# A scan and attention kernel on one core: the second norm with tokens on partitions, b and c in two parts, one product on another engine, weights loaded in parts, new orders

## What is computed

```
mod = (silu(c) @ wmod).reshape(16, 6, 1, 256);  sa, ca, ga, sb, cb, gb = mod[:, 0..5]
h = layernorm(x) * (1 + ca) + sa
xz = h @ W_in.T;  xs, z = split(xz)                      # 512 channels each
B, C = xs @ W_B.T, xs @ W_C.T                            # 16 states each
dt = softplus(xs @ W_dt.T + b_dt)
state[t] = exp(dt[t] * A) * state[t-1] + dt[t] * B[t] * xs[t]      # 512 channels x 16 states
y = (sum over states of state * C + xs * D) * silu(z)
x1 = x + ga * (y @ W_out.T) * sigmoid(output_gate)
h2 = layernorm(x1) * (1 + cb) + sb                       # "the second norm"
for l in 0, 1: h2 = attention layer(h2)                  # qkv, rotary, 128-wide windows, wo,
                                                         # shifted layernorm, w1, gelu gate, w2
out = x1 + gb * h2
```

## Time and profile before

| | |
|---|---|
| median of 3 runs | 4182.83 us (4182.79 to 4183.98) |
| the profiled execution, its own time | 4186.23 us |
| its span, first to last instruction | 4184.4 us, 61077 instructions |
| busy: PE / DVE / ACT / POOL | 95% / 87% / 66% / 64% of the span |
| scan phase | 40 to 1751 us |
| second phase | 1752 to 4184 us |
| mean granted clock of PE | 0.982 of full speed |

### The profile page before, as it was taken

The page is one execution under the profiler, slowest core; times in us unless marked ns, Lnnn a source line. Parts: engine busy times, 40 slices in busy tenths (PEclk is TensorE's granted clock), DMA queues, the critical chain, the costliest instruction groups (busy, mean ns, idle before and its releaser), DMA issues.

```text
span 4184.4 us, 61077 instructions
## 1 busy us (share of the span) xinstructions
PE 3982.3 (95%) x19870; PEld 2670.8 (64%) x19870; DVE 3624.9 (87%) x6114; ACT 2743.5 (66%) x5896; POOL 2670.3 (64%) x1298
## 2 busy tenths in 40 slices
PE   7999999999999999769999999999999999999997
PEld 4444444444444444347887778787777878777785
DVE  5999999999999999768888888877888887878884
ACT  6677777777777775336767676666767666666764
POOL 3999999999999999553434444443534444343442
PEclk8999999999999999879999999999999999999998
DMA  3333333333333333420000000001110101000010
GB/s 109 117 124 124 122 122 121 122 121 121 122 122 123 125 122 116 137 91 27 21 26 17 31 16 31 16 31 51 36 63 21 41 21 37 26 31 32 21 36 26
DMA packets 119610, 295.11 MB, mean 71 GB/s; under 512 B 21288, under 2 KB 45664, under 8 KB 119296
## 3 DMA queue, kind: packets, MB, share of 16 engines
q1 hardware_dynamic: 117424, 291.15, 21.1%
q10 hardware_dynamic: 1872, 0.05, 0.0%
HBM read 248.52 MB, written 42.64 MB: 70 GB/s over the span
## 4 chain that ended last, share of the span: by engine, by line
PE 51%; DVE 2%; ACT 1%; DMA 1%; issue 1%; POOL 1%; SPq 0%; DVEq 0%; ACTq 0%; POOLq 0%
PE b_bank L1346 12%; PE b_bank L1474 12%; PE b_bank L1495 6%; PE b_bank L1425 5%; PE b_bank L1398 5%; PE b_bank L1409 5%; PE b_bank L1439 4%; PE b_bank L1378 3%; DMA b_hx<-stack_rows 1%; PE b_bank L1446 1%; ACT b_probs_t L1586 0%; DVE b_hx_part L1728 0%; DVE b_qk_rot L1773 0%; PE b_bank L1510 0%; POOL b_scores L1704 0%
## 5 line engine op out<-in xcount | busy, mean ns | idle before, releaser
L824 POOL TENSOR_TENSOR a_state<-a_state,a_c_wide 128x1024 f32<-128x1024 f32 x512 | 1195.1, 2371 | 19.7 <-DVE a_state L766 19.7
L1704 POOL TENSOR_TENSOR b_scores<-b_scores,b_row_rate 128x1024 f32<-128x1024 f32 (+1 forms) x256 | 458.2, 1801 | 825.6 <-DVE b_row_rate L1825 825.6
L584 PE MATMUL a_y_sum<-a_state,a_ident 128*128 128x512 f32 x2048 | 951.2, 597 | 6.8 <-POOL a_state L824 6.8
L766 DVE TENSOR_TENSOR_SCAN a_state<-a_decay,a_slot 128x1024 f32<-128x1024 f32 x352 | 788.7, 2270 | 0.7
L1346 PE MATMUL b_bank<-b_w_qkv,b_hx_part 128*128 128x512 f32 x2304 | 604.8, 408 | 29.9 <-DVE b_hx_part L1728 9.1
L584 PEld LDWEIGHTS a_y_sum<-a_state,a_ident 128*128 128x128 f32 x2048 | 387.3, 191 | 383.0 <-issue 316.7
L1677 POOL TENSOR_TENSOR b_by_cos<-b_qk,b_rotary 128x1024 f32<-128x1024 f32 x128 | 310.2, 2424 | 475.5 <-DVE b_qk L1757 473.4
L1474 PE MATMUL b_bank<-b_hn_part,b_w 128*128 128x512 f32 x2112 | 526.2, 399 | 7.0 <-DVE b_hn_part L1728 6.9
L695 ACT ACTIVATE a_decay<-a_dt,a_neg_a 128x512 f32<-128x512 f32 x704 | 453.8, 710 | 114.5 <-DVE a_state L766 114.1
L1574 ACT ACTIVATE b_scores<-b_scores,b_row_bias 128x256 f32<-128x256 f32 (+1 forms) x1024 | 478.2, 472 | 69.4 <-DVE b_row_bias L1814 69.4
L1346 PEld LDWEIGHTS b_bank<-b_w_qkv,b_hx_part 128*128 128x128 f32 x2304 | 428.3, 192 | 128.8 <-issue 16.4
(11 more groups left out here) (211 smaller groups left out, 6946.2 us busy)
## 6 DMA issues: line engine op xcount, KB each, us to landing
a_c_wide<-bc_rows SPq DMA_DIRECT2D x256, 512.0 KB, 3.8
a_b_wide<-bc_rows SPq DMA_DIRECT2D x80, 512.0 KB, 4.8
b_hx<-stack_rows SPq DMA_DIRECT2D x64, 256.0 KB, 3.9
b_x_res<-stack_rows SPq DMA_DIRECT2D x32, 512.0 KB, 3.4
a_xt<-in_L_attn_x SPq DMA_DIRECT2D x16, 512.0 KB, 5.4
x_rows<-a_x_t SPq DMA_DIRECT2D x16, 512.0 KB, 5.4
stack_rows<-a_h_t SPq DMA_DIRECT2D x16, 512.0 KB, 5.3
stack_rows<-b_xc SPq DMA_DIRECT2D x16, 512.0 KB, 2.9
```

Source lines behind the costliest of these rows:

```text
L584: last = nc.tensor.matmul(y_sum[dd][:], ident[:], state[state_ring.slot[q]][:, i, :], start=False, stop=(j == GROUPS - 1 and i == GROUP - 1))
L766: nc.vector.tensor_tensor_scan(flat(h), flat(factor), flat(term), 0.0, ALU.mult, ALU.add).then_inc(scan_done.sem, 1)
L824: nc.gpsimd.tensor_tensor(h[:], h[:], c_wide[c_ring.slot[q // 2]][:], ALU.mult).then_inc(cmul_done.sem, 1)
L1704: nc.gpsimd.tensor_tensor(probs, probs, row_rate[:, w, at].unsqueeze(2).to_broadcast([P, 4, hi - lo]), ALU.mult)\
```

## The change

1. **The second norm** has tokens on partitions now. PE turns x1 in PSUM (`turn_tail`, sixteen 128-column transposes for both ways), ScalarE copies with an accumulated sum (`copy_tail`), squares with an accumulated sum, takes ln and exp of a 128x4 tile (`statistics_tail`) and normalises (`normalise_tail`); PE turns back (`turn_back_tail`), ScalarE modulates from PSUM. The averages on PE and both VectorE passes are gone.
2. **b and c in two fp32r parts**, 64 rows: `bcrest` and `bcmid` are gone, `picks` is fp32r.
3. **Unit 9** is made by VectorE (TO_VECTOR): its b is spread by PE, its decay goes to SBUF. Unit 8, of the same load, stays on GpSimd.
4. **The cut of dt** moves from GpSimd to ScalarE (step `cut`).
5. **The first norm** works in place in xt: it waits until x is turned, and the first sequence's normalisation comes behind the setup's barrier.
6. **Second phase:** the q, k and v thirds of layer 1's weights are loaded one by one, each when the last product of layer 0 with that third is done; w_1 and w_2 are loaded in `load_hx` of sequence 18, behind its hx. ORDER, BANK_OF, FIRST_ORDER and MIXER_ORDER are new.

```diff
...
+TO_VECTOR = 9
...
-    for part in range(3):
+    for part in range(2):
...
-    1: "xload xT xcopy stat norm hT mod up hcut xs xscopy bc bccopy cstore bcup bcrest bcmid bclow dt soft dtadd"
-       " z zcopy silu",
+    1: "xload xT xcopy stat norm hT mod up hcut xs xscopy bc bccopy cstore bcup bclow dt soft dtadd"
+       " z zcopy silu cut",
     0: "skip bcast cload bload decay mul scan cmul sum gate",
-    -1: "out res x1store mean2 cen2 sq2 var2 dev2 xn2 h2 h2store"}
+    -1: "out res x1store turn2 tot2 stat2 norm2 hT2 h2 h2store"}
...
-scan-:10 scan-:11 cmul-:6 cmul-:7 scan-:12 scan-:13 bcast-:13 bcmid-:0 xT-:1 xs-:0 xscopy-:3 xs-:1 decay-:19 soft-:0
...
+mul-:28 sum-:27 decay-:24 mul-:29 decay-:25 decay-:26 cmul-:26 bcast-:31 scan-:28 xload:0 sum-:28 cmul-:27 dt-:1
...
-        picks = sb("picks", [P, STATES, P], BF16)
+        picks = sb("picks", [4 * STATES, STATES, P])
...
-        by_pool = [q for q in units if q // 2 in POOL_LOADS]
+        by_pool = [q for q in units if q // 2 in POOL_LOADS and q != TO_VECTOR]
...
-            normalise_head_of(act, 0)
...
+            wait(act, x_turned, s, CHUNKS)
             wait(act, shift_done, s, TILES)
             for t in range(TILES):
-                nc.scalar.activation(xn[:, t, :], xt[:, t, :], ACT.Identity, bias=token_shift[:, t:t + 1],
+                nc.scalar.activation(xt[:, t, :], xt[:, t, :], ACT.Identity, bias=token_shift[:, t:t + 1],
                                      scale=token_rate[:, t:t + 1]).then_inc(xn_done.sem, 1)
...
-                    last = nc.tensor.matmul(slots[q % 2][:, i, :], picks[0:96, GROUP * j + i, :], bc_parts[slot][0:96, :],
+                    last = nc.tensor.matmul(slots[q % 2][:, i, :], picks[:, GROUP * j + i, :].bitcast(F32R), bc_parts[slot][:].bitcast(F32R),
...
+            def turn_tail(s, slot, i):
                 wait(pe, x1_done, s, CHUNKS)
...
+                banks.wait_free(pe, s, f"turn2{i}")
+                for t in (2 * i, 2 * i + 1):
+                    for c in range(CHUNKS):
+                        at = (t % 2) * DIM + c * P
+                        last = nc.tensor.transpose(bank(f"turn2{i}")[:, at:at + P], x1_t[:, c, t * P:(t + 1) * P], ident[:])
+                last.then_inc(x1_turned.sem, 1)
+
+            def turn_back_tail(s, slot, c):
+                wait(pe, xn2_done, s, TILES)
+                banks.wait_free(pe, s, f"hT2{c}")
+                for t in range(TILES):
+                    last = nc.tensor.transpose(bank(f"hT2{c}")[:, t * P:(t + 1) * P], xn2[t][:, c * P:(c + 1) * P], ident[:])
+                last.then_inc(h2_turned.sem, 1)
...
+                nc.scalar.activation(bc_parts[slot][0:2 * STATES, :].bitcast(F32R), bank("bc0")[0:2 * STATES, :], ACT.Copy).then_inc(parts_upper.sem, 1)
...
+            def cut(s, slot, half):
+
+                wait(act, u_done, s, half + 1)
+                nc.scalar.activation(dt[slot][:, 2 * half:2 * half + 2, 0:1], half_cut[:], ACT.Copy, scale=2.0).then_inc(dt_done.sem, 1)
...
+            def copy_tail(s, slot, i):
+                wait(act, h2_turned, s - 1, CHUNKS)
+                wait(act, x1_turned, s, i + 1)
+                for t in (2 * i, 2 * i + 1):
+                    at = (t % 2) * DIM
+                    nc.scalar.activation(xn2[t], bank(f"turn2{i}")[:, at:at + DIM], ACT.Copy, accum_out=neg_mean2[:, t:t + 1])\
+                        .then_inc(total2_done.sem, 1)
+
+            def statistics_tail(s, slot, _):
                 wait(act, h2_stored, s - 1, 1)
...
+                wait(act, total2_done, s, TILES)
+                nc.scalar.activation(neg_mean2[:], neg_mean2[:], ACT.Copy, scale=-1.0 / DIM).then_inc(mean2_done.sem, 1)
+                wait(act, mean2_done, s, 1)
+                for t in range(TILES):
+                    nc.scalar.activation(squares2[t], xn2[t], ACT.Square, bias=neg_mean2[:, t:t + 1],
+                                         accum_out=token_rate2[:, t:t + 1]).then_inc(var2_done.sem, 1)
+                wait(act, var2_done, s, TILES)
+                nc.scalar.activation(token_rate2[:], token_rate2[:], ACT.Ln, scale=1.0 / DIM, bias=ln_eps[:]).then_inc(var2_done.sem, 1)
+                wait(act, var2_done, s, TILES + 1)
+                nc.scalar.activation(token_rate2[:], token_rate2[:], ACT.Exp, scale=-0.5).then_inc(rate2_done.sem, 1)
+
+            def normalise_tail(s, slot, _):
+                wait(act, rate2_done, s, 1)
...
+            def modulate_tail(s, slot, c):
+                wait(act, h2_turned, s, c + 1)
+                modulate(s, h2_t[:, c, :], bank(f"hT2{c}"), MOD_SHIFT_B, MOD_SCALE_B, c).then_inc(h2_done.sem, 1)
...
+            def lower_bc(s, slot, _):
+                wait(dve, bc_done, s, 1)
                 wait(dve, parts_upper, s, 1)
...
+                nc.vector.tensor_tensor(bc_parts[slot][2 * STATES:, :].bitcast(F32R), bank("bc0")[0:2 * STATES, :],
+                                        bc_parts[slot][0:2 * STATES, :], ALU.subtract).then_inc(parts_done.sem, 1)
...
-                wait(pool, u_done, s, half + 1)
-
-                nc.gpsimd.tensor_tensor(dt[slot][:, pair, 0:1], half_cut[:], half_cut[:], ALU.add).then_inc(dt_done.sem, 1)
...
-ptr-:3 v-:3 hxs:0 mask:1.0 vc-:3 mask:1.1 score:0.0 score:0.1 score:1.0 hxload:0 exp:0 rate:0 add:0 pss:0 score:1.1
...
+onorm-:3 ptr-:3 att-:3 mask:0.0 mask:0.1 score:0.0 score:0.1 score:1.0 exp:0 psq:0 score:1.1 hxs:0 hxload:0 mask:1.0
...
-pss:0 pnorm:0 prot:0 padd:0 pq:0 pk:0 v:0 pss:1 psq:0 prate:0 vc:0 psq:1 prate:1 ptc:0 pnorm:1 pk:1 prot:1 vc:1 vc:2
...
+pq:0 psq:0 pk:0 pss:0 pnorm:0 prate:0 vc:0 prot:0 v:0 psq:1 prate:1 padd:0 pss:1 pnorm:1 vc:1 pk:1 prot:1 v:1 pq:1
...
-            def load_qkv():
-
-                for i, done in enumerate(qkv_loaded):
-                    at = slice(i * INNER, (i + 1) * INNER)
-                    for to, source in zip(w_qkv, parts_dram["qkv"]):
-                        sp.dma_start(to[:, :, at], source[:, :, at]).then_inc(done, 16)
+            def load_qkv(i):
+
+                at = slice(i * INNER, (i + 1) * INNER)
+                for to, source in zip(w_qkv, parts_dram["qkv"]):
+                    sp.dma_start(to[:, :, at], source[:, :, at]).then_inc(qkv_loaded[i], 16)
...
-                if s < 3 or s == BATCH:
+                if s < 3:
...
-                    load_qkv()
+                    sp.wait_ge(q_full.sem, q_full.at(s - 1, TILES))
+                    load_qkv(0)
+                    sp.wait_ge(k_full.sem, k_full.at(s - 1, TILES))
+                    load_qkv(1)
+                    sp.wait_ge(v_done.sem, v_done.at(s))
+                    load_qkv(2)
                     sp.wait_ge(by_cos_done.sem, by_cos_done.at(s))
                     sp.wait_ge(by_sin_done.sem, by_sin_done.at(s))
                     sp.dma_start(rotary[:], rotary_dram).then_inc(rotary_moved, 16)
+                if s == BATCH + 2:
+                    sp.wait_ge(h2_done.sem, h2_done.at(BATCH))
+                    load_w_1()
+                    sp.wait_ge(x_out_done.sem, x_out_done.at(BATCH))
+                    for to, source in zip(w_2, parts_dram["w_2"]):
+                        sp.dma_start(to[:], source).then_inc(w_2_loaded, 16)
...
-                if s == BATCH - 1:
-                    sp.wait_ge(h2_done.sem, h2_done.at(BATCH))
-                    for done, group in zip(moved, (early, late)):
-                        sp.wait_ge(done, 3 * loads_of(group))
-                    load_w_1()
                 sp.wait_ge(x_out_done.sem, x_out_done.at(s, CHUNKS))
                 sp.dma_start(stack_dram[s + BATCH], x_out[:]).then_inc(stored.sem, 16)
-                if s == BATCH - 1:
-                    for to, source in zip(w_2, parts_dram["w_2"]):
-                        sp.dma_start(to[:], source).then_inc(w_2_loaded, 16)
...
-                nc.vector.tensor_copy(picks[0:96], pick[0:96].unsqueeze(2).to_broadcast([96, STATES, P]))
+                nc.vector.tensor_copy(picks[:].bitcast(F32R), pick[0:4 * STATES].unsqueeze(2).to_broadcast([4 * STATES, STATES, P]))
...
```

192 lines of the change are left out of this document (74 added, 118 removed).

## The result

| | before | after |
|---|---|---|
| median of 4 runs | 4182.81 us | 4239.38 us (4233.92 to 4242.63) |
| the profiled execution's span | 4184.4 us | 4240.8 us |
| interval of a sequence | 103.33 us | 109.77 us |
| first to last logarithm of the second phase's norm, 31 intervals | 2233.4 us | 2190.0 us |

The ratio is 1.0135, 95% interval 1.0117 to 1.0152: slower by 56.6 us, where I forecast 41 us less. The two traces say where (times of the two profiled executions, spans 56.4 us apart): the first Silu starts 4.3 us later, fifteen sequences take 96.6 us more, the last Silu to the first product of the second phase 3.4 more; then the second phase gives back 3.9 at its start, 43.4 in 31 passes and 0.6 at its end.

The account below looks back on a forecast made before the run. VectorE, with GpSimd level, was taken to bound the scan phase, TensorE the second. Terms -23 + 4.5 - 8.3 - 2.5 - 3 - 6 - 2 = -40.3 from 4186.2 us, less 3.4 to the median: 4142 us, range 4114 to 4172.

Parts of the forecast that it names:

- the waits for spreads: Scan phase, sign of being wrong: VectorE waits for spreads or decays by more than 0.5 us per sequence.
- the step of 0.3: Scan phase, sign of being wrong: TensorE's fp32r spreads step by more than 0.3 us.
- the longer passes: Second phase, sign of being wrong: passes take longer than 71.7 us.
- Rival D: Scan phase: TensorE becomes the bound, slower from a spread step of 0.335 us; at 0.43, +66 us, 4231; chance 0.07.
- Scan phase, VectorE: VectorE, without slack at 103.3 us per sequence, loses norm passes and a subtraction, gains a product: net -1.7, to 101.6.
- Its gain of 1.43 us per sequence: Scan phase: the interval falls by 1.73 us less 0.3 of new waits, times 16 sequences: -23 us.
- rival A: Scan phase: later spreads or decays hold VectorE another 1.4 us per sequence, taking the 23 us gain: 4165; chance 0.15.
- GpSimd: Scan phase: GpSimd falls from about 103 to 100.2 us per sequence, no longer level with VectorE, which sets the interval.
- Ends of the scan phase: First normalisation +3.3, path through b and c -1.9, longer serial ScalarE norm about +3: +4.5 us (0 to +9).
- Weights, -8.3 and -2.5: Second phase: stall at layer 1's q, k, v load gone, -8.3 us; wait for hx behind w_1 and w_2, -2.5.
- Orders: Second phase's new order: -3 us for hx waits, -6 for the mean's wait for probabilities, -2 in the first pass.
- B: Second phase rival: the new order costs one microsecond in each of 32 passes and the mean's 6: 4180; chance 0.10.

Follow-up runs that it names:

- e1: The changed kernel with the spread of b padded from 64 to 96 rows with zeros, still fp32r: 4136.84 us, 0.9888 of before.
- e5: e1 with one of the three products of the scan phase's two-part projections left out: 4141.57 us, 0.9904 of before.
- e3: The kernel before with the whole new second phase (orders, banks, weight loads): 4135.09 us, 0.9884 of before.
- e6: e1 with the product of unit 9 back on GpSimd: 4166.55 us, 0.9966 of before.
- e8: The kernel before with only the second phase's new orders and banks, old weight loads: 4134.61 us, 0.9885 of before.
- e4: The kernel before with only the new loads of layer 1's weights, old orders: 4175.54 us, 0.9981 of before.
- e9: The changed kernel, still 64 rows, with the pattern and the two parts of b in bf16: 4191.57 us, 1.0022 of before.

## Why the prediction was wrong, step by step

- **The step that failed**: "How an fp32r spread with 64 rows and a 0/1 pattern steps is in no row. Lower bound 0.215, upper bound 0.43, I take 0.24." The product does step by 0.235. Missing is the term for the two ends of each stretch, 0.20 and 0.19 us. I had read the length of the load (187 ns) and charged 0.05 for its later end; what counts is where it starts. TensorE's work rose by 7.5 us per sequence, where I had no rise (98.8 to 98.7), and its room before was 3.6 us and not 4.5. Of the signs that I had named, the waits for spreads came (5 us per sequence, where 0.5 was the mark); the step of 0.3 and the longer passes did not.
- **Rival D** was this outcome in its mechanism (TensorE becomes the bound), its place and nearly its time (4231 against 4239), with 0.07. I argued against it with fp32r products "at full width and depth", which is just what a 64-row spread is not. Its price was put on the product instead of on the change of height, so its threshold of 0.335 could not be judged from any row. That its time came so near is luck: it had 70 us of loss in the scan phase and 22 of gain in the second, where 104 and 48 were measured.
- **Scan phase, VectorE**: the sums were right. In e1, where height is taken out, VectorE's steps at their medians add up to 101.5 us, as forecast: both norm passes and one subtraction gone, one product more.
- **Its gain of 1.43 us per sequence** did not come even in e1: 103.40. VectorE's idle time rose from 0.3 to 1.2 us per sequence, where I charged 0.3 more, and some of its steps came out longer than the median. That is rival A, once height is out of the way; what holds it there is open after e5. So the scan phase's rewrite, even without the 64 rows, gained nothing: e3, with the scan phase of before, takes 4135.09 us and e1 4136.84.
- **GpSimd** fell below VectorE as forecast (101.57 of 110 busy after). I took the moved product as a cost to VectorE that GpSimd's relief merely allowed; e6 shows it to be worth 2.1 us in the new order.
- **Ends of the scan phase**: +4.5 forecast, +7.7 measured: 4.3 at the first Silu instead of 1.4, 3.4 at the end instead of 3. Neither bears out its term. Before, e3 and e8 share one scan phase, and their first Silu starts at 68.2, 69.8 and 70.8 us, so up to 2.6 of the 4.3 can be spread between runs. And in e1 the end, from the last Silu to the first product of the second phase, takes 136.1 us against 137.1 before: the 3.4 goes with the height, and the 3 for ScalarE's longer norm met it by luck.
- **Weights, -8.3 and -2.5**: e4 gives -8.2 for both with the old orders; how that divides between them no trace shows. With the new orders the stall would have been gone anyway. I added two edits that remove the same wait.
- **Orders**: -3 for hx, -6 for the mean, -2 for the start, 11 in all; e8 shows 47 with the stall's 8 in it. Small waits for hx fell from 5.8 to 0.6 us and the mean's waits went, near the forecast. What I did not count is what a busy TensorE hides: 0.4 us per pass in exposed loads at the scores, and 0.26 in the row of sixteen turns besides the wait behind it. (Ahead of the mean stand sixteen score products, not the eight of the prediction.) I had written that in the second phase "only what TensorE waits for counts", with 74.75 of 75 busy; loads that are not covered count as busy there.
- **The chances**: half of B's 0.10 is 0.05, where the sum took 0.04; it changes nothing.

## What to carry to other kernels

Lay the row of weight loads beside the row of products and compare starts, not lengths: a load that starts with its product can be on the path, and the steps on both sides, added up, say whether it is. Do this wherever the height or the width of neighbouring products differs, and price a change of shape by what stands before and behind it; padding with zero rows can be the faster form. On an engine that a page shows as 99% busy there can still be one per cent of exposed loads and short waits (0.96 of 71.7 us per pass here), and a handmade order with a fixed map of banks loses them again with one step moved. Test each part of a change by itself: here one part lost 102 us, another gained 47, and a third gained nothing.

## What the runs showed of the hardware

- Products of 64 rows between products of 128: load exposed at both ends, 0.20 us at the start and 0.19 at the end in fp32r, 0.10 and 0.19 in bf16 (e9). Each end costs about the load that stands there: the spread's own at the start (185 ns in fp32r, 94 in bf16), that of the fp32 sums behind it at the end (190). 96 rows among 128: not exposed, in bf16 or in fp32r (e1). Further products of the stretch are not charged. Into products of 128 rows that are 64 columns wide the load starts with its product too (second phase of before). The load's length does not depend on the height: 185 ns for 64 rows, 190 for 96 and for 128 in fp32r and fp32. On that the Trainium skill agrees, in "TensorE: Matmul & The Clock Gate", section on LDWEIGHTS: columns count, not rows. Its section "The mechanism" says that a load is pulled ahead when its row group does not conflict or when it goes to the background weight buffer, and in its list of what overlaps it says that a load overlaps with running products only when the row groups differ. The rows here differ from that list: between 128-row products in the same rows the load leads by 0.23 us, and it is at a change to or from 64 rows that it does not. Why 64 rows prevent it and 96 do not, no run here shows.
- With 6 us less work per sequence, and idle for 12 of 200 us instead of 6.6, TensorE was granted a lower clock in the scan phase (0.97 for 0.99, more stretches at 1.2 GHz among those at 2.4), and the kernel was not faster (e5).
